# A lambda layer on one core: the sums of a half go through DRAM, with one store and four loads in place of sixteen transfers between partitions

## What is computed

```
h = relu(bn(conv1x1(gn(x), conv1_w)))                 # 512 -> 128 channels
q = bn(conv1x1(h, q_w)); k = softmax(conv1x1(h, k_w)); v = bn(conv1x1(h, v_w))
content_lambda = einsum('bkm,bvm->bkv', k, v)
pos = conv(v, emb)                                    # 15 x 15 windows, 16 of them
out = einsum('bhkn,bkv->bhvn', q, content_lambda) + einsum('bhkn,bkvn->bhvn', q, pos)
h = relu(bn(out))                                     # 4 heads x 32 = 128 channels
y = relu(bn(conv1x1(h, conv3_w)) + gn(x));  result = x + y
```

## Time and profile before

| | us |
|---|---|
| median of three executions | 5223.5 |
| lowest, highest | 5221.0, 5228.1 |
| the profiled execution | 5228.7 |
| its span (first to last instruction) | 5227.0 |
| TensorE busy | 4672.8 (89%) |
| VectorE busy | 2957.6 (57%) |
| ScalarE busy | 2282.6 (44%) |
| GpSimd busy | 748.4 (14%) |
| mean granted clock of TensorE | 0.926 |

### The profile page before, as it was taken

The page is one execution under the profiler, slowest core; times in us unless marked ns, Lnnn a source line. Parts: engine busy times, 40 slices in busy tenths (PEclk is TensorE's granted clock), DMA queues, the critical chain, the costliest instruction groups (busy, mean ns, idle before and its releaser), DMA issues.

```text
span 5227.0 us, 121426 instructions
## 1 busy us (share of the span) xinstructions
PE 4672.8 (89%) x49366; PEld 2740.0 (52%) x49366; DVE 2957.6 (57%) x4695; ACT 2282.6 (44%) x2816; POOL 748.4 (14%) x433
## 2 busy tenths in 40 slices
PE   4899999899999899999899999999988999999897
PEld 2555555555455555555555555455555555555454
DVE  4465565565555565545656556556556555556553
ACT  1444444444444454444444444444444444445443
POOL 0011110111111111101111111111111111011111
PEclk8898999999999999999989998999999899989998
DMA  3678766678666787666786667876667876678765
GB/s 97 190 237 280 239 212 233 232 251 282 216 213 232 239 271 257 196 227 233 250 278 206 218 229 238 281 243 210 243 225 251 281 233 200 236 234 266 262 192 201
DMA packets 540244, 1217.09 MB, mean 233 GB/s; under 512 B 54312, under 2 KB 236588, under 8 KB 539820
## 3 DMA queue, kind: packets, MB, share of 16 engines
q1 hardware_dynamic: 474348, 950.15, 56.1%
q10 hardware_dynamic: 65472, 260.05, 14.0%
HBM read 777.68 MB, written 365.22 MB: 219 GB/s over the span
## 4 chain that ended last, share of the span: by engine, by line
PE 50%; issue 12%; DVE 12%; DMA 8%; SPq 7%; ACT 7%; POOL 2%; ACTq 0%; DVEq 0%; POOLq 0%
PE ring L498 13%; PE ring L643 13%; PE ring L517 9%; PE ring L573 6%; SPq L387 5%; DMA h<-S 4%; PE ring L597 4%; DMA X<-x_dram 3%; PE ring L524 2%; POOL X L1166 2%; ACT region L782 2%; PE ring L607 2%; DVE S L1010 2%; DVE ring L1014 2%; DVE region L965 2%
## 5 line engine op out<-in xcount | busy, mean ns | idle before, releaser
L691 ACT COPY region<-ring 126x1024 f32<-126x1024 f32 x1184 | 1163.2, 1015 | 1137.4 <-PE ring L498 1127.9
L573 PE MATMUL ring<-h,w3T 128*128 128x512 f32 x2048 | 1016.3, 637 | 130.7 <-DVE S L1010 82.1
L517 PE MATMUL ring<-X,w1e 128*128 128x512 f32 x2048 | 911.0, 598 | 49.7 <-DVE w1e L887 28.9
L498 PE MATMUL ring<-Qt,Ep 96*126 96x256 bf16 x5120 | 851.4, 308 | 101.3 <-ACT region L691 65.7
L643 PE MATMUL ring<-region,V 126*32 126x128 f32 x24576 | 875.2, 287 | 20.4 <-issue 20.4
L498 PEld LDWEIGHTS ring<-Qt,Ep 96*126 96x126 bf16 x5120 | 626.6, 152 | 346.9 <-issue 171.2
L643 PEld LDWEIGHTS ring<-region,V 126*32 126x32 f32 x24576 | 675.0, 115 | 240.6 <-issue 230.1
L691 DVE COPY region<-ring 126x1024 f32<-126x1024 f32 x352 | 430.1, 1222 | 630.7 <-PE ring L498 630.7
L863 DVE BATCH_NORM_STATS2 st<-X 128x6 f32<-128x512 f32 x1024 | 624.6, 677 | 207.2 <-DMA X<-x_dram 207.1
L573 PEld LDWEIGHTS ring<-h,w3T 128*128 128x128 f32 x2048 | 381.2, 199 | 570.2 <-issue 366.9
L517 PEld LDWEIGHTS ring<-X,w1e 128*128 128x128 f32 x2048 | 382.4, 190 | 527.9 <-issue 478.2
(11 more groups left out here) (127 smaller groups left out, 3069.5 us busy)
## 6 DMA issues: line engine op xcount, KB each, us to landing
X<-x_dram SPq DMA_DIRECT2D x132, 2048.0 KB, 21.0
out_dram<-X SPq DMA_DIRECT2D x512, 512.0 KB, 9.9
X<-x_dram ACTq DMA_DIRECT2D x124, 2048.0 KB, 9.4
Qt<-q_parts SPq DMA_DIRECT2D x768, 128.0 KB, 4.1
V<-v_windows SPq DMA_DIRECT2D x96, 1024.0 KB, 8.2
h<-S SPq DMA_DIRECT2D x1024, 64.0 KB, 2.0
q_parts<-region SPq DMA_DIRECT2D x128, 256.0 KB, 3.2
v_windows<-region SPq DMA_DIRECT2D x64, 512.0 KB, 5.8
```

Source lines behind the costliest of these rows:

```text
L498: last = nc.tensor.matmul(dst[0:TROWS, i * 256:(i + 1) * 256], taps(u, xo, yo), Q[:, :, xo * BLK + yo, :], start=(i % 2 == 0), stop=True, ...
L517: last = nc.tensor.matmul(dst[:, hh * HALF:(hh + 1) * HALF], w1e[:, c, :], X[:, j, c, hh * HALF:(hh + 1) * HALF], start=(c == 0), stop=(c ...
L573: last = nc.tensor.matmul(dst[:, yb * HALF:(yb + 1) * HALF], w3T[:, t, :], src, start=True, stop=True)
L691: return engine_copy(dst, src)
```

## The change

`shuffle` stores the half S as it stands to a new tensor in DRAM (hD), with one transfer of 128 partitions by 8 KB. SyncE waits for it to land (h_out), and then issues four loads, one for each head, each into 32 partitions with four pieces of 2 KB. The loads raise h_in, four times 16 per half instead of sixteen times. Whoever waited for S to be read (the sums of the second half, and VectorE's first use of T) now waits for the store alone; ScalarE's L710 waits for the loads.

```
+        hD = nc.dram_tensor("lambda_sums", (2, NCH, DV, HEADS, HALF), F32, kind="Internal").ap()
...
+        h_out = [sem(f"h_out{i}") for i in range(2)]
...
             def shuffle(b, i):
                 sp.wait_ge(sum_by_act, b * 4 + 2 * i + 2)
                 sp.wait_ge(sum_by_dve, b * 4 + 2 * i + 2)
-                for c in range(NCH):
-                    for h in range(HEADS):
-                        sp.dma_start(h2[h * DV:(h + 1) * DV, c, i, :], S[c * DV:(c + 1) * DV, h, :]).then_inc(h_in[i], 16)
+                sp.dma_start(hD[i].rearrange("c v h n -> (c v) (h n)"), S[:, :, :].rearrange("p h n -> p (h n)"))\
+                    .then_inc(h_out[i], 16)
+                sp.wait_ge(h_out[i], b * 16 + 16)
+                for h in range(HEADS):
+                    sp.dma_start(h2[h * DV:(h + 1) * DV, :, i, :], hD[i, :, :, h, :].rearrange("c v n -> v c n"))\
+                        .then_inc(h_in[i], 16)
...
             def bn2_relu(b, j):
                 if j == 0:
                     for i in range(2):
-                        act.wait_ge(h_in[i], b * 256 + 256)
+                        act.wait_ge(h_in[i], b * 64 + 64)
...
-                        act.wait_ge(h_in[0], b * 256 + 256)
+                        act.wait_ge(h_out[0], b * 16 + 16)
...
-                        dve.wait_ge(h_in[0], b * 256 + 256)
+                        dve.wait_ge(h_out[0], b * 16 + 16)
...
-                        dve.wait_ge(h_in[1], b * 256 + 256)
+                        dve.wait_ge(h_out[1], b * 16 + 16)
```

## The result

The changed kernel takes 5178.8 us in the median of four executions (5162.6 to 5191.6), against 5225.8 (5221.0 to 5228.8) of the kernel before, four executions as well. The ratio is 0.991, with an interval of 0.989 to 0.993. So it is faster by about 0.9%, 47 us where 58 were forecast; the time lies in the range, 14 us above the predicted 5165. In a second comparison, with fifteen executions of the kernel before, it took 5179.0 against 5236.4: a ratio of 0.988 (0.987 to 0.990), and 57 us less.

What follows compares the result with a forecast made beforehand. Two paths of nearly equal length, h2's transfers and TensorE's work, bound the kernel; 31 x 1.8 + 2.5 = 58 us off 5228.7 gives 5170.5, and the median 5.2 lower gives 5165 us (-1.1%), range 5120 to 5215.

Steps and rivals of the forecast that it cites:

- What a sooner h2 gives: TensorE's idle time between k0 and c2 in the 31 inner images: 1.8 us per image can be had, not 16.
- The limit of 14.4 us: Latest start of L710 after the store's issue (2150.3 on the image's clock) that still gives the full 1.8 us.
- later costs one for one: Each us that h2 lands past the limit delays c2 by one us.
- The store: One 1 MB store from 128 partitions replaces sixteen issues and lands 3.9 us after its issue, at 2139.8.
- that rival: Late store puts the loads behind ScalarE's reload: h2 at 2154, loss of 64 us, 5287 us; 8%, standstill between 9%.
- The loads: Four loads issued 0.64 us apart, ahead of the reload, the last taking 6.5 us: h2 at 2148.3.
- The lower bound: Earliest h2, 2144.7, with the loads flowing alone in just under 3 us.
- The port rule: 32 neighbouring partitions reach 8 of 16 ports, about 218 GB/s: 1 MB in 4.8 us, h2 2150.5, gain 1.6 us.
- The standstill by a slow store: Store of about 5.6 us lands h2 at 2152 as today, 5213 to 5234 us; 9%. Skill's 6.15 us gives about 5230.
- Half 0, and the q store: SyncE's new wait for h_out costs nothing in half 0 and doesn't delay the next image's q store.
- The freed queue: SyncE reaches the loads of V some 2 us sooner beyond the shift, X follows: 20 us more, 5145 us; 12%.
- The last image: No next image covers the transfers there: 11.5 us become 8.8 plus 0.1, a gain of about 2.5 us.

Runs made afterwards that it cites:

- the two kernels with small transfers: Kernel before with ScalarE's reload moved behind L710, plus 8 or 11 unread 16 KB transfers ahead of half 1's sixteen; 5184.9 and 5226.0 us.
- the kernel with the second store: Changed kernel with the same store once more, to a tensor nobody reads, between store and loads of half 1; 5360.9 us, 1.023.
- the one load into 128: Changed kernel with the DRAM layout turned round: four stores from 32 partitions each, then one load into all 128; 5176.5 us, 0.988.
- Half 0 alone: Changed kernel with only half 0 through DRAM, half 1 again with sixteen transfers; 5234.9 us, 1.000.
- eleven small transfers: Kernel before with the reload behind L710 and eleven unread 16 KB transfers ahead of half 1's sixteen; 5226.0 us, 0.998.
- eight: Kernel before with the reload behind L710 and eight unread 16 KB transfers ahead of half 1's sixteen; 5184.9 us, 0.990.
- the six kernels at the floor: The change, half 1 alone, later reload, sixteen on two queues, loads on two queues, four stores with one load; c0 to c2 681.4, 5168.8 to 5179.6 us.

## Why the prediction was right, and where its steps were off

**What a sooner h2 gives: right in kind and size.** 1.8 us per image was read from one image and from two rows of waits; 1.82 came, 56.3 us in all against the 56 in the sum. The limit of 14.4 us was read from the kernel before; the two kernels with small transfers, late in another way, give 14.3. That "later costs one for one" holds to 2 us beyond it, and is too mild at 5.

**The store: right.** 3.9 us in the median, from the nearest row. Of L387 (first line, issue to landing) and of L391, the loads, in both halves (second line):

```profile
DMA to landing us min/median/max: 3.8/3.9/5.8
```
```profile
DMA to landing us min/median/max: 3.7/5.2/6.8
```

The 5.8 is of a half 0; all 32 stores of half 1 land in 3.9. So the point of 5.6 from which that rival decides (the prediction doesn't show how it is worked out) was never near.

**The loads: right enough in the sum, wrong in the working.** I had them 0.64 us apart, the spacing of L387; that belongs to the transfers between partitions, and the loads went out 0.34 to 0.47 apart, the last 0.6 us sooner. I had taken 2.6 us for their flow when alone, and 6.5 for the last, as for transfers caught by the reload. In the traced image they landed 3.85, 4.58, 5.28 and 5.99 us after their own issues, 1.1 to 1.2 us one from the next: a plain flow at the pace of 32 partitions, in which the reload, issued 3 us after the first load, plays no visible part. h2 at +11.2 instead of +12.4, and either is before 14.4. The lower bound was the part that was plainly wrong: it took its rate from stores out of all partitions, which move twice as fast.

**The port rule: right, and I added it to the wrong thing.** The Trainium skill's page SBUF — State Buffer, "Door 1: The DMA port swizzle", gives about 218 GB/s for a range of 32 partitions. I wrote that no row showed it, and didn't build on it; the runs show 208 to 237 for 32 partitions and 407 to 434 for all, in agreement with it. From it I had worked out h2 at +14.6 and a gain of 1.6 us per image, and that didn't come. Its 4.8 us for the megabyte agree with the trace (4.6 us, from 2.7 after the first issue, if the first load flows for 1.15 us like the others, to 7.3). What was wrong was that I put the extra 2.2 us on top of 6.5 us for the last load, which had the reload's delay in it, and that delay didn't come. Where it does come, behind the reload in the kernel with the second store, the four loads take 11.5 us from their first issue instead of 7.3.

**The standstill by a slow store.** The Trainium skill's DMA: Bandwidth & Descriptors, section Bandwidth, has 6.15 us for a megabyte, from HBM into 128 partitions and issued from GpSimd; the prediction took it for a store, which goes the other way, issued from SyncE. The trace has 3.9 for this store out of 128 partitions and 5.5 for the one load into 128; the measurement decides. The two stores of 512 KB in the earlier trace rows were the better guide.

**Half 0, and the q store: right.** Half 0 alone costs and gives nothing in c0 to c2, and 1.000 in time. The new wait of SyncE is the fifth of its waits in all (the longest, 1171.3 us, is for the sums themselves), and no store of queries goes out later for it: the first stands at 2142.20, 22.8 us after c0, and stood 27.0 us after it. SyncE's queue (us in total, times, longest):

```profile
SPq L391 <- DMA lambda_sums<-S: 224.4, 64, 5.5
```

**The freed queue: false.** I gave it 12%, on the thought that SyncE would reach the loads of V sooner than the shift alone. They are issued 52.0 us after c2 in the mean of the inner images, 51.8 before. The waits between hang on others: the store of the queries of chunk 2 stands at 2170.47, when GpSimd has made them, and TensorE's order sets that. VectorE's wait for X fell only from 207.1 to 199.1:

```profile
  DMA X<-x_dram: 199.1, 32
```

**The last image: the term that was mis-sized.** 2.5 us forecast, 0.4 measured. The timeline's end answers to the earlier trace rows:

```profile
5134.88 0.34 SPq L387 DMA_DIRECT2D lambda_sums<-S  x1
...
5138.75 1.73 SPq L391 DMA_DIRECT2D h<-lambda_sums  x4
...
5146.00 4.63 ACT L715 ACTIVATE h<-h,pbi,psc 128x1024 f32<-128x1024 f32 x4 [12.17 <-DMA h<-lambda_sums]
5147.29 18.26 PE L578 MATMUL ring<-h,w3T 128*128 128x512 f32 x38 [13.21 <-ACT h L715]
```

11.1 us from issue to L715, where 11.5 were before and 8.9 forecast. No reload is near and no next image covers the loads, so their rate is the whole matter: they take 7.2 us where I had 4.9 with their issues. The row of 2.6 us, with the rate of stores from 128 partitions behind it, was the wrong one. The expected sign was right. The wait before L710 "of about 9 us" is one of 12.2, and TensorE's behind it one of 13.2 where it was 13.6.

**What came back.** The forecast of 58 us took the other stages as fixed. Two of them aren't. From the first weights of the next position part to its products, the sum is 541 in the kernel before and with half 0 alone, 540 with the second store, 534.5 with eleven small transfers, 544 with eight, and 547 to 552 in the seven traces with h2 at 11.5 us or sooner: some 8 of the 56 us are given back there whenever they are gained. It goes with the time that TensorE stands at the low level in it: 5.5 us per image with eleven small transfers, 5.9 to 6.3 in the kernel before, half 0 alone, the second store and eight small transfers, 6.7 to 7.1 in the seven. Why that depends on h2 isn't settled by these runs. The other, the first half of the position part, goes from 1156 to 1176 us among kernels that don't differ in it, and with no order in their h2, a single traced execution of each; it was 1166.3 before and 1176.5 after. That is of the size of the 20 us that the range allowed for. Of the 14 us between forecast and result, 2.3 are the kernel before, whose median was 5225.8 here and 5223.5 when the forecast was made, 2.1 are the last image, and the 8 us and this spread cover the rest. Against the kernel before of their own batch, the six kernels at the floor gain 57 to 68 us, around the forecast of 58.

## What to carry to other kernels

A share of the chain that ended last is no price. Here 9% of it was worth 1%, since another path of nearly the same length ran beside it; what is to be had is read at the meeting point, as the idle time of the engine that two paths feed, and past it a sooner arrival (7.7 us or 11.5) gives nothing at all. Before a route is rebuilt, see what the late ones are late for: five of sixteen transfers waited behind a 2 MB reload, and issuing that one step later gave the whole gain with none of the bytes through DRAM. And a time that follows the stretch in question may still be off elsewhere: two kernels here came out 20 us faster than their stretch says, with a higher granted clock. Take the pace of a transfer from a row with as many partitions, not only as many bytes: a store from 128 partitions and a load into 32 differ by two.

## What the runs showed of the hardware

- **A large transfer issued just ahead, on another engine's queue, holds the small ones behind it.** Transfers of 64 KB between partitions land 2.0 us after issue ahead of the 2 MB reload, 5.3 to 6.5 behind it, and 2.0 when it is moved away. With the second store the loads behind it need 7.2 to 10.1 us instead of 3.9 to 6.0. Of the six loads of queries of chunk 0 in the changed kernel (2146.44 to 2149.65, the reload at 2148.54), three issued 0.8 us ahead of it and more land in 2.6 to 2.7 us; one issued 0.2 us ahead lands in 6.1, and the two behind in 7.3 and 7.8. The loads of h2 issued 1.7 us ahead of a reload and more aren't visibly held.
- **The price of an issue depends on its shape.** On SyncE's queue, transfers between partitions take 0.63 us from one to the next, the loads 0.47, the small ones of 16 KB 0.46, the one store of 1 MB 0.34 alone.
- **32 partitions move half of what 128 do**, in both directions: 208 to 237 GB/s against 407 to 434, with the DMA engines full in both. Two transfers to different halves of the partitions, on two queues, come to 328 for one microsecond and then to 247. Transfers between partitions, 32 wide, are as slow by packet (137 ns for 2 KB), so DRAM isn't it. The single packets say how: 150 ns for 2 KB, where 84 do with 128 partitions.
- **A gap costs more than itself once TensorE's clock falls.** After 3.5 us of waiting the conv3 tiles take 6.8 us, where 3.67 is their time at 2.4 GHz. The stretch of 6.7 us from there has a granted clock of 0.54, close to the low level; the kernel before, with 0.3 us of waiting at the same place, has 1.00. Over the 31 stretches from c0 to c2 TensorE stands at the low level for 5.5 us each with the second store, and for none in the kernel before.
